# Attention and feed-forward block, one core: the FFN's first scale before the transposes of its tokens, one FFN tile before a V unit, evictions behind taps, and the next statistics in halves 4 and 5

## The chip, the cores and the metric

One core of a Trainium2 chip runs the whole block. The metric is the device time of an execution in microseconds, as the median of several runs. The engines are TensorE (PE in the profile, PEld its weight loads), VectorE (DVE), ScalarE (ACT), GpSimd (POOL) and SyncE (SP, which issues the DMAs); each runs its own list of instructions in order, and they wait on each other by semaphores.

## What is computed

64 sequences of 128 tokens and 256 channels pass cross-attention with a context of 192 channels (16 heads of 64; LoRA terms added to the weights; the last 4 context tokens have keys, values and a softmax of their own), then a feed-forward part with activations quantised to 8 bits and ternary weights.

```python
q_in = x @ Wq + lora(x);  k_in = org_ctx @ Wk + lora(org_ctx);  v_in = org_ctx @ Wv + lora(org_ctx)
out = attention(q_in, k_in, v_in) + attention(q_in, ipa_ctx @ Wk_ipa, ipa_ctx @ Wv_ipa)
x = x + (out @ Wo + bo + lora(out))              # of layernorm(x)
h = bit_linear(layernorm(x), w1)                  # 256 -> 1024; activations round(x*127/max|x|)
h = silu(depthwise_conv1d(h, conv_w) + conv_b)    # 3 taps along the tokens
x = x + bit_linear(h, w2)                         # 1024 -> 256
```

## The kernel before

The sequences go in 16 groups of 4 (NB = 4, so T = 512 tokens a group). Work is a software pipeline of passes; pass g has 32 halves, numbered n = 0 to 31. Pass g runs the attention of group g (one chunk of 4 heads and 1 sequence in every two halves: scores, softmax, transposes of the probabilities, p_v, output projection), the projections of group g+1 (functions `project`; the last of them, n + 32, lie in halves 0 to 7 of the next pass), and the feed-forward part of group g-1 (functions `finish`; its end, n + 32, lies in the pass after). Passes 0 and 1, and 15 to 17, are written out; 2 to 14 are a loop. The last group has its own `finish_last`.

Each engine has its own `steps(g, n)`, which calls the parts of half n in a fixed order; that order and the table of halves at the head of the file (N_... for projections, M_... for the feed-forward part) are all that sets the order of instructions. On TensorE a half is: on even n the four parts of the attention, then `project`, then `finish`. On ScalarE: on even n the copies of the attention's output and of the transposed probabilities, then `project`, then `finish`, then on even n the exponentials. On VectorE: on even n the sums of the chunk before, a copy of V, on even n the maxima, then `finish` of group g-2, `project`, `finish` of group g-1.

What the change touches:
- Layernorm of x: VectorE takes BN_STATS of XIN (line 877, two sequences a half, N_STATS), aggregates in half N_VAR = 5, POOL takes the power in half 6, VectorE normalises in half 7 (line 856). In halves 1 to 3 VectorE also scales and rounds the second activations (lines 1086, 1090).
- The first scale and the tokens' transposes: the bank psF is used in turn for the transposes of the quantised tokens Q1 (line 576, half M_QT = 13; ScalarE copies them into Q1T, line 764), for the transposes that lay the scales out along the tokens (line 582, half M_BC1 = 14; copied into BC, line 771), and then for the eight FFN tiles. The group before uses it until VectorE's line 1025 of half 11 (semaphore fin_done).
- The FFN tiles (line 591, halves 15 + M_TILE) all use psF: tile j waits until VectorE has evicted tile j-1 with BC as factor (line 1062, g_done). ScalarE then scales it into HT (line 777), VectorE adds the tap of the token before (conv_before, line 1003) and of the token behind (conv_next, line 997), ScalarE takes the tanh (line 782), VectorE the gate (line 1009).
- Units are projections of one tile: Q (line 443), K (452), V (462). p_v is line 478, the transposes of the probabilities are line 487, the scores 500, the output projection 513, the second FFN product 612. Softmax: maxima lines 913 and 914 and line 916 on VectorE, exponentials 751 and 754 on ScalarE, sums 906 and 908 on VectorE, product 1238 on POOL. POOL also runs lines 1269 and 1276.

In pass 6, which the rows below show, half 0 starts at 586.04 us, half 4 at 594.58, half 12 at 618.73, half 16 at 630.78, half 20 at 642.35 and half 28 at 662.70 (the first matmul of p_v in each); pass 7 starts at 675.10.

Of the kernel before, what the change touches and what calls it, by code (L numbers as in the profile page):

```python
# [44 lines left out]
CT = HID // P  # L45
# [8 lines left out]

N_STATS, N_VAR, N_POW, N_NORM = 0, 5, 6, 7
N_XT = 8
# [13 lines left out]
M_POW, M_NORM = 9, 9  # L70
M_QT, M_BC1 = 13, 14
M_F1 = 15
M_TILE = (0, 1, 2, 4, 5, 6, 8, 9)
M_LAG = (1, 1, 2, 3, 3)
M_HOFF = 4
M_HMAX = M_F1 + M_TILE[-1] + M_HOFF
M_HT, M_BC2 = M_HMAX + 2, M_HMAX + 4
# [69 lines left out]
def program(nc, x, ctxT, cipaT, Wq, Wk, Wv, Wo, bo, q_downT, q_up, k_downT, k_up, v_downT, v_up, o_downT, o_up,  # L147
            alphas, Wk_ipa, Wv_ipa, w1T, conv_w, conv_b, w2T, out):
    with ExitStack() as ctx:
# [269 lines left out]
        def _(pe):  # L419
# [146 lines left out]
            def finish(g, n):  # L566
# [3 lines left out]
                if n == M_QT:  # L570
                    pe.wait_ge(q1_done, g.count(1, 1))
                    need(pe, fin_done, g.count(2, 0))
                    bank = psF.bitcast(BF16).rearrange("p (k b t) -> p k b t", k=2, b=NB)
# [4 lines left out]
                if n == M_BC1:  # L578
                    pe.wait_ge(scale_done, g.count(2, 1))
                    pe.wait_ge(q1t_done, g.count(1, 1))  # L580
                    for b in range(NB):
                        m = pe.transpose(psF[:, TOK * b:TOK * b + TOK], AD[0][:, b:b + 1].broadcast_to([P, P]), IDF[:])
                    m.then_inc(bc_full, 1)
                j = tile_at(n - M_F1)
                if 0 <= j < CT:
                    if j == 0:
                        pe.wait_ge(bc_done, g.count(1, 1))
                    else:
# [89 lines left out]
            def steps(g, n):  # L678
# [8 lines left out]
                if g.reg is None:  # L687
                    ternary(g, n)
                if g.exists():
                    project(g, n + HALVES)  # L690
                if g.shift(1).exists(1):
                    project(g.shift(1), n)
                if g.shift(-2).exists():
                    finish(g.shift(-2), n + HALVES)
                if g.shift(-1).exists():
                    finish(g.shift(-1), n)
# [144 lines left out]
        def _(dve):  # L841
# [173 lines left out]
            def finish(g, n):  # L1015
# [30 lines left out]
                if n == M_NORM + M_SCALE:  # L1046
# [6 lines left out]
                    dve.wait_ge(q1_scaled, g.count(1, 1))  # L1053
                    dve.tensor_scalar(Q1, XN2, MAGIC, None, ALU.subtract).then_inc(q1_done, 1)
                j = tile_at(n - M_F1)
                if 0 <= j < CT:
# [5 lines left out]
                    dve.tensor_tensor(GB[j % 4].rearrange("p b t -> p (b t)"), psF, BC[:], ALU.mult).then_inc(g_done, 1)  # L1062
                j = tile_at(n - M_F1 - M_LAG[2])
                if 0 <= j < CT:
                    conv_next(g, j)
                j = tile_at(n - M_F1 - M_LAG[1])
                if 0 <= j < CT:
                    conv_before(g, j)
                j = tile_at(n - M_F1 - M_LAG[4])
# [254 lines left out]
```

## Time and profile before

| | |
|---|---|
| median of 3 runs | 1536.86 us (1536.23 to 1538.49) |
| profiled execution, its own time | 1535.5 us |
| its span, first to last instruction | 1533.5 us |
| TensorE busy | 1409.5 us, 92% |
| VectorE busy | 1195.5 us, 78% |
| ScalarE busy | 1182.3 us, 77% |
| POOL busy | 668.1 us, 44% |
| chain that ended last | TensorE 43%, VectorE 30%, ScalarE 17%, issue 9% |

The chain is followed back from the last instruction, at each step to what released it. Its shares say how long each engine set the end; "issue" is time in which an engine waited for nothing that the profile shows. Busy time of TensorE is modelled from pipelined matmuls, so starts are safer than ends. Times in the rows are us from the start of the span.

### The profile page before, as it was taken

To read this page: it belongs to the slowest core of one execution; us is meant where nothing else is said; L and a number is where in the kernel's file an instruction comes from. 1 tells how busy PE (TensorE), PEld (TensorE's weight loads), DVE (VectorE), ACT (ScalarE), POOL (GpSimd) and SP (SyncE) were. 2 spreads that over 40 slices of the span, in tenths; PEclk is the share of its full clock that TensorE was granted. 3 is DMA by queue.
4 is the path that set the end of the run, shared out by engine and by line. 5 is a ranking of instruction groups with operands and counts; after the bars stand their busy time and mean duration, and the time that the engine had idled before them with its cause. 6 is when DMAs were issued, how large, how long until landed. Compare 5 with 4: busy or idle time off the path is not lost.

```text
span 1533.5 us, 33070 instructions
## 1 busy us (share of the span) xinstructions
PE 1409.5 (92%) x10604; PEld 1159.5 (76%) x10650; DVE 1195.5 (78%) x3059; ACT 1182.3 (77%) x3909; POOL 668.1 (44%) x1058
## 2 busy tenths in 40 slices
PE   7899999999999999999999999999999999999762
PEld 4688778787777878777787878788787777878541
DVE  4363698787969878796887878688787878788888
ACT  3477787978878797887879788787978788797832
POOL 2354444445444444544544454444445444444420
PEclk9999999999999999999999999999999999999985
DMA  9210100000010100000010000001000000100000
GB/s 279 53 31 16 31 16 28 20 28 30 24 34 15 33 11 28 30 28 29 15 44 1 29 28 28 29 15 44 8 23 28 28 29 15 44 1 1 29 15 14
DMA packets 41144, 47.13 MB, mean 31 GB/s; under 512 B 3024, under 2 KB 35216, under 8 KB 41104
## 3 DMA queue, kind: packets, MB, share of 16 engines
q1 hardware_dynamic: 41104, 46.62, 10.1%
q8 instruction: 22, 0.36, 0.1%
q14 instruction: 18, 0.15, 0.0%
HBM read 36.13 MB, written 10.49 MB: 30 GB/s over the span
## 4 chain that ended last, share of the span: by engine, by line
PE 43%; DVE 30%; ACT 17%; issue 9%; DMA 1%; DVEq 0%; POOL 0%; SPq 0%; POOLq 0%; ACTq 0%
PE PS L500 10%; ACT SM L751 8%; PE PS L462 6%; PE PS L443 5%; PE PS L513 5%; PE PS L478 4%; PE PS L487 4%; PE PS L452 3%; PE PS L591 2%; DVE HP L1003 2%; DVE GBS L1062 2%; DVE MX L914 2%; DVE GBS L1086 2%; DVE HP L1009 2%; ACT QM L719 2%
## 5 line engine op out<-in xcount | busy, mean ns | idle before, releaser
L1238 POOL TENSOR_TENSOR SM<-SM,RC 128x496 f32<-128x496 f32 (+1 forms) x512 | 324.2, 654 | 738.6 <-DVE RC L908 738.6
L751 ACT ACTIVATE SM<-PS,MX 128x124 f32<-128x124 f32 x1024 | 359.9, 367 | 159.1 <-DVE SM L916 155.8
L500 PE MATMUL PS<-KT,QM 128*128 128x128 f32 x2048 | 278.1, 279 | 24.0 <-ACT SM L751 24.0
L500 PEld LDWEIGHTS PS<-KT,QM 128*128 128x128 f32 x2048 | 249.4, 192 | 38.6 <-ACT SM L751 38.1
L751 ACT ACTIVATION_READ_ACCUMULATOR SM<-PS,MX 128x1 f32 x1024 | 212.2, 207 | 0.0
L1269 POOL TENSOR_TENSOR OTl<-OF,OTh 128x256 fp32r<-128x256 f32 x256 | 204.1, 797 | 10.4 <-ACT OF L745 10.4
L487 PE MATMUL PS<-IDF,SM 128*128 128x128 f32 x1024 | 168.4, 287 | 16.6 <-POOL SM L1238 16.5
L743 ACT ACTIVATE OTh<-PS 128x256 fp32r<-128x256 f32 x256 | 100.4, 392 | 93.5 <-PE PS L478 92.5
L914 DVE TENSOR_REDUCE MX<-PS 128x4 f32<-128x496 f32 x256 | 170.5, 666 | 0.4 <-issue 0.4
L478 PEld LDWEIGHTS PS<-PT,V 128*64 128x64 f32 x2048 | 106.6, 136 | 82.3 <-issue 75.4
L478 PE MATMUL PS<-PT,V 128*64 128x128 f32 x2048 | 168.6, 286 | 0.0
L737 ACT ACTIVATE PT<-PS 128x512 f32<-128x512 f32 x256 | 157.4, 615 | 0.3 <-PE PS L487 0.3
L487 PEld LDWEIGHTS PS<-IDF,SM 128*128 128x128 f32 x1024 | 107.8, 141 | 63.1 <-issue 35.3
L1062 DVE TENSOR_TENSOR GBS<-PS,BC 128x512 f32<-128x512 f32 x120 | 82.5, 688 | 89.6 <-PE PS L591 88.6
L1009 DVE SCALAR_TENSOR_TENSOR HP<-GBS,HP 128x512 f32<-128x512 f32 x128 | 111.6, 872 | 22.0 <-ACT GBS L782 21.0
L513 PE MATMUL PS<-WOh,OTh 128*128 128x256 f32 x512 | 123.5, 322 | 0.7 <-POOL OTl L1269 0.7
L777 ACT ACTIVATE HP<-GBS,CB,CW 128x512 f32<-128x512 f32 x128 | 112.8, 882 | 10.0 <-DVE GBS L952 5.0
L913 DVE TENSOR_REDUCE MX<-PS 128x4 f32<-128x16 f32 x256 | 40.4, 158 | 100.6 <-PE PS L500 99.0
L997 DVE SCALAR_TENSOR_TENSOR HP<-GBS,CW,HP 128x508 f32<-128x508 f32 x128 | 110.0, 860 | 0.1
L443 PE MATMUL PS<-XTh,WQh 128*128 128x512 f32 x256 | 107.3, 419 | 0.0
L1003 DVE SCALAR_TENSOR_TENSOR HP<-GBS,CW,HP 128x508 f32<-128x508 f32 x128 | 97.3, 760 | 11.8 <-ACT HP L777 11.8
L745 ACT ACTIVATE OF<-PS 128x256 f32<-128x256 f32 x256 | 100.8, 394 | 5.4 <-POOL OTl L1269 5.4
(166 smaller groups left out, 3511.5 us busy)
## 6 DMA issues: line engine op xcount, KB each, us to landing
XIN<-in_x SPq DMA_DIRECT2D x16, 512.0 KB, 3.5
XRES<-in_x SPq DMA_DIRECT2D x16, 512.0 KB, 4.6
out_y<-HP SPq DMA_DIRECT2D x15, 512.0 KB, 3.2
CRAW<-in_ctxT SPq DMA_DIRECT2D x16, 256.0 KB, 2.7
RRAW<-in_ctxT SPq DMA_DIRECT2D x32, 128.0 KB, 2.9
QM<-in_Wq SPq DMA_DIRECT2D x1, 1024.0 KB, 9.1
GBS<-in_Wo SPq DMA_DIRECT2D x1, 1024.0 KB, 14.0
k_ipa_columns<-HP SPq DMA_DIRECT2D x1, 1024.0 KB, 6.5
```

The costliest lines, as they stand in the source:

```text
L443: m = mm(bank, WQ[w][:, k, P * tile:P * tile + P], XT[xt][:, k, :], start=(i == 0), stop=(i == 5))
L478: m = mm(psO[r:r + DH, h // 2, :], V[:, b, DH * (4 * q + h):DH * (4 * q + h) + DH], PT[:, h, :], start=True, stop=True)
L487: m = pe.transpose(psT[:, h, :], SM[c % 2][:, h, :], IDF[:])
L500: m = mm(psS[:, h, :], QM[:, 2 * q + h // 2, h % 2, TOK * b:TOK * b + TOK], KT[:, 2 * q + h // 2, b, :], start=True, stop=True)
L513: m = mm(psY[b // 2][:, b % 2, :], OT[ot][c % 2][:, a, :], WO[w][:, 2 * q + a, :], start=(q == 0 and i == 0 and b % 2 == 0), stop=(q == QU ...
L737: act.activation(PT[:], psT, ACT.Identity).then_inc(pt_done, 1)
L751: m = act.activation(SM[s % 2][:, h, 0:ORG], psS[:, h, 0:ORG], ACT.Exp, bias=MX[s % 2][:, h:h + 1], accum_out=SU[s % 2][:, h:h + 1])
L914: dve.tensor_reduce(MX[s % 2][:, 0:4], psS[:, :, 0:ORG], AX.X, ALU.max, negate=True)
L1003: dve.scalar_tensor_tensor(out=y[:, :, 1:TOK], in0=GB[j % 4][:, :, 0:TOK - 1], scalar=CW[:, j, 0:1], in1=y[:, :, 1:TOK], op0=ALU.mult, op1 ...
L1009: dve.scalar_tensor_tensor(out=y, in0=GB[j % 4], scalar=1.0, in1=y, op0=ALU.add, op1=ALU.mult).then_inc(h_done, 1)
L1238: m = pool.tensor_tensor(part, part, RC[c % 2][:, 4 * i:4 * i + 4].unsqueeze(2).broadcast_to(shape), ALU.mult)
L1269: pool.tensor_tensor(OT[1][c % 2][:], OF[:], OT[0][c % 2][:].bitcast(F32), ALU.subtract).then_inc(ot_done, 1)
```

## The change

Four edits to the order. The layout of the scales moves from half 14 to 12 (M_BC1), ahead of the tokens' transposes in 13, and the waits follow: the scales' transposes now wait for fin_done, the tokens' transposes for bc_done, the first tile for q1t_done. ScalarE's copy of BC follows to half 13, since it stands at M_BC1 + 1. In half 16 (M_AHEAD) TensorE runs `finish`, that is tile 1, ahead of `project`, the V unit. On VectorE the eviction of a tile stands behind conv_next and conv_before of the same half. BN_STATS of the next x moves from halves 0 and 1 to 4 and 5 (N_STATS).

```diff
--- before.py
+++ after.py
@@ -52,7 +52,7 @@
 U_Q, U_K, U_V = (0, 3), (1, 4), (2, 5)
 
 
-N_STATS, N_VAR, N_POW, N_NORM = 0, 5, 6, 7
+N_STATS, N_VAR, N_POW, N_NORM = 4, 5, 6, 7
 N_XT = 8
 N_CIN = 7
 N_CSPLIT = 8
@@ -68,11 +68,12 @@
 M_X2 = (4, 7)
 M_STATS = 7
 M_POW, M_NORM = 9, 9
-M_QT, M_BC1 = 13, 14
+M_QT, M_BC1 = 13, 12
 M_F1 = 15
 M_TILE = (0, 1, 2, 4, 5, 6, 8, 9)
 M_LAG = (1, 1, 2, 3, 3)
 M_HOFF = 4
+M_AHEAD = (16,)
 M_HMAX = M_F1 + M_TILE[-1] + M_HOFF
 M_HT, M_BC2 = M_HMAX + 2, M_HMAX + 4
 M_Q2 = M_HMAX + 5
@@ -569,7 +570,7 @@
                     return
                 if n == M_QT:
                     pe.wait_ge(q1_done, g.count(1, 1))
-                    need(pe, fin_done, g.count(2, 0))
+                    pe.wait_ge(bc_done, g.count(1, 1))
                     bank = psF.bitcast(BF16).rearrange("p (k b t) -> p k b t", k=2, b=NB)
                     for k in range(2):
                         for b in range(NB):
@@ -577,14 +578,14 @@
                     m.then_inc(q1t_full, 1)
                 if n == M_BC1:
                     pe.wait_ge(scale_done, g.count(2, 1))
-                    pe.wait_ge(q1t_done, g.count(1, 1))
+                    need(pe, fin_done, g.count(2, 0))
                     for b in range(NB):
                         m = pe.transpose(psF[:, TOK * b:TOK * b + TOK], AD[0][:, b:b + 1].broadcast_to([P, P]), IDF[:])
                     m.then_inc(bc_full, 1)
                 j = tile_at(n - M_F1)
                 if 0 <= j < CT:
                     if j == 0:
-                        pe.wait_ge(bc_done, g.count(1, 1))
+                        pe.wait_ge(q1t_done, g.count(1, 1))
                     else:
                         pe.wait_ge(g_done, g.count(CT, j))
                     for k in range(2):
@@ -686,13 +687,15 @@
                         project_out(g, 3)
                 if g.reg is None:
                     ternary(g, n)
+                if n in M_AHEAD and g.shift(-1).exists():
+                    finish(g.shift(-1), n)
                 if g.exists():
                     project(g, n + HALVES)
                 if g.shift(1).exists(1):
                     project(g.shift(1), n)
                 if g.shift(-2).exists():
                     finish(g.shift(-2), n + HALVES)
-                if g.shift(-1).exists():
+                if n not in M_AHEAD and g.shift(-1).exists():
                     finish(g.shift(-1), n)
 
             run_groups(pe, steps)
@@ -1052,6 +1055,12 @@
                     m.then_inc(q1_scaled, 1)
                     dve.wait_ge(q1_scaled, g.count(1, 1))
                     dve.tensor_scalar(Q1, XN2, MAGIC, None, ALU.subtract).then_inc(q1_done, 1)
+                j = tile_at(n - M_F1 - M_LAG[2])
+                if 0 <= j < CT:
+                    conv_next(g, j)
+                j = tile_at(n - M_F1 - M_LAG[1])
+                if 0 <= j < CT:
+                    conv_before(g, j)
                 j = tile_at(n - M_F1)
                 if 0 <= j < CT:
                     dve.wait_ge(f1_full, g.count(CT, j + 1))
@@ -1060,12 +1069,6 @@
                     if j >= 4:
                         dve.wait_ge(h_done, g.count(CT, j - 3))
                     dve.tensor_tensor(GB[j % 4].rearrange("p b t -> p (b t)"), psF, BC[:], ALU.mult).then_inc(g_done, 1)
-                j = tile_at(n - M_F1 - M_LAG[2])
-                if 0 <= j < CT:
-                    conv_next(g, j)
-                j = tile_at(n - M_F1 - M_LAG[1])
-                if 0 <= j < CT:
-                    conv_before(g, j)
                 j = tile_at(n - M_F1 - M_LAG[4])
                 if 0 <= j < CT:
                     gate(g, j)
```

VectorE at the start of a pass in the loop, from the end of half 0's softmax to the sums of half 2 (line 877 is BN_STATS, 906 the sums; in the changed file they are lines 880 and 909). Before:

```order
L916 TENSOR_TENSOR SM<-PS,MX 128x4x4
L875 REGISTER_ALU
L877 BN_STATS BS<-XIN 128x6 x2
L1083 ISA
L1086 TENSOR_TENSOR GBS<-HP,PS 128x512 x4
L1088 ISA
L1090 TENSOR_SCALAR HP<-GBS 128x512 x2
L1088 REGISTER_ALU
L1090 TENSOR_SCALAR HP<-GBS 128x512 x2
L877 BN_STATS BS<-XIN 128x6 x2
L906 TENSOR_REDUCE SU<-SM 128x4
```

Now:

```order
L919 TENSOR_TENSOR SM<-PS,MX 128x4x4
L1086 ISA
L1089 TENSOR_TENSOR GBS<-HP,PS 128x512 x4
L1091 ISA
L1093 TENSOR_SCALAR HP<-GBS 128x512 x2
L1091 REGISTER_ALU
L1093 TENSOR_SCALAR HP<-GBS 128x512 x2
L909 TENSOR_REDUCE SU<-SM 128x4
```

Both pairs of BN_STATS have left this stretch; they stand behind the softmax of half 4 and behind the copy of V in half 5.

ScalarE from the copy of Q1T in half 14 to the copy of BC in half 15 before (764 and 771), and from the exponentials of half 12 to the copy of Q1T in half 14 now (754, 774, 767). Before:

```order
L764 ACTIVATE Q1T<-PS 128x1024
L749 REGISTER_ALU
L751 ACTIVATE SM,SU<-PS,MX 128x124 x4
L754 ACTIVATE SM<-SM 128x4x4
L717 REGISTER_ALU
L718 ACTIVATE QM<-PS 64x512
L719 ACTIVATE QM<-PS 64x512
L769 ISA
L131 REGISTER_ALU
L771 ACTIVATE BC<-PS 128x512
```

Now:

```order
L754 ACTIVATE SM,SU<-PS,MX 128x124 x4
L757 ACTIVATE SM<-SM 128x4x4
L772 ISA
L132 REGISTER_ALU
L774 ACTIVATE BC<-PS 128x512
L746 ACTIVATE OTh<-PS 128x256
L748 ACTIVATE OF<-PS 128x256
L740 ACTIVATE PT<-PS 128x512
L767 ACTIVATE Q1T<-PS 128x1024
```

The copy of BC now stands right behind the exponentials of half 12, ahead of the copies of half 14; it stood behind the exponentials of half 14 and two copies of Q.

VectorE in halves 16 and 17, behind the softmax of half 16 (evictions 1062, now 1071; tap before 1003, now 1006; tap behind 997, now 1000). Before:

```order
L916 TENSOR_TENSOR SM<-PS,MX 128x4x4
L1057 REGISTER_ALU
L1062 TENSOR_TENSOR GBS<-PS,BC 128x512
L1003 SCALAR_TENSOR_TENSOR HP<-GBS,CW,HP 128x4x127
L1057 REGISTER_ALU
L1062 TENSOR_TENSOR GBS<-PS,BC 128x512
L997 SCALAR_TENSOR_TENSOR HP<-GBS,CW,HP 128x4x127
L1003 SCALAR_TENSOR_TENSOR HP<-GBS,CW,HP 128x4x127
```

Now:

```order
L919 TENSOR_TENSOR SM<-PS,MX 128x4x4
L1006 SCALAR_TENSOR_TENSOR HP<-GBS,CW,HP 128x4x127
L1066 REGISTER_ALU
L1071 TENSOR_TENSOR GBS<-PS,BC 128x512
L1000 SCALAR_TENSOR_TENSOR HP<-GBS,CW,HP 128x4x127
L1006 SCALAR_TENSOR_TENSOR HP<-GBS,CW,HP 128x4x127
L1066 REGISTER_ALU
L1071 TENSOR_TENSOR GBS<-PS,BC 128x512
```

The eviction of tile 1 moved behind one tap, that of tile 2 behind two.

## Rows read from the trace of the kernel before

**Rows 1.** The chain in order of time, passes 6 to 7: start, us, what.

```profile
605.04 0.17 DVE MX L913
...
645.68 0.49 DVE GBS L1062
...
651.78 0.07 ACT SM L751
```

**Rows 2.** Timeline of PE, one pass; in brackets idle us before, and its releaser.

```profile
624.83 1.16 PE L500 MATMUL PS<-KT,QM 128*128 128x128 f32 x8 [0.25 <-ACT SM L751]
...
630.47 0.38 PE L591 MATMUL PS<-Q1T,W 128*128 128x512 bf16 x1 [0.78 <-ACT BC L771]
...
636.02 0.60 PE L591 MATMUL PS<-Q1T,W 128*128 128x512 bf16 x2 [0.79 <-DVE GBS L1062]
...
663.70 0.66 PE L487 MATMUL PS<-IDF,SM 128*128 128x128 f32 x4 [0.34 <-POOL SM L1238]
...
665.18 1.16 PE L500 MATMUL PS<-KT,QM 128*128 128x128 f32 x8 [0.83 <-ACT SM L751]
...
684.78 0.66 PE L487 MATMUL PS<-IDF,SM 128*128 128x128 f32 x4 [0.49 <-POOL SM L1238]
...
685.77 1.16 PE L500 MATMUL PS<-KT,QM 128*128 128x128 f32 x8 [0.33 <-ACT SM L751]
```

**Rows 3.** Timeline, VectorE in halves 0 to 6: start, us, engine, line, op, out<-in.

```profile
588.97 0.74 DVE L877 BATCH_NORM_STATS2 BS<-XIN 128x6 f32<-128x256 f32 x2
...
593.35 0.76 DVE L877 BATCH_NORM_STATS2 BS<-XIN 128x6 f32<-128x256 f32 x2
...
594.01 0.16 DVE L906 TENSOR_REDUCE SU<-SM 128x4 f32<-128x16 f32 x1
...
605.04 0.17 DVE L913 TENSOR_REDUCE MX<-PS 128x4 f32<-128x16 f32 x1 [3.05 <-PE PS L500]
```

**Rows 4.** Timeline of all engines, halves 12 to 15.

```profile
621.33 0.87 DVE L1025 SCALAR_TENSOR_TENSOR HP<-PS,AD,HP 128x256 f32<-128x256 f32 x2
...
621.61 0.28 PE L462 MATMUL PS<-WVh,CTh 128*128 128x256 f32 x1
...
622.78 0.62 PE L576 MATMUL PS<-IDB,GBS 128*128 128x128 bf16 x8
...
624.66 0.22 ACT L754 ACTIVATE SM<-SM 128x16 f32<-128x16 f32 x1
...
627.93 0.60 PE L582 MATMUL PS<-IDF,AD 128*128 128x128 f32 x4
...
629.59 0.60 ACT L771 ACTIVATE BC<-PS 128x512 f32<-128x512 f32 x1
```

**Rows 5.** Timeline of ScalarE and VectorE, halves 16 to 20.

```profile
636.00 0.87 ACT L777 ACTIVATE HP<-GBS,CB,CW 128x512 f32<-128x512 f32 x1
...
638.33 0.85 ACT L777 ACTIVATE HP<-GBS,CB,CW 128x512 f32<-128x512 f32 x1
...
641.21 1.23 DVE L1009 SCALAR_TENSOR_TENSOR HP<-GBS,HP 128x512 f32<-128x512 f32 x1
...
643.73 0.68 DVE L1009 SCALAR_TENSOR_TENSOR HP<-GBS,HP 128x512 f32<-128x512 f32 x1
```

**Rows 6.** Timeline of PE: half 28 of pass 14, half 4 of passes 7, 15.

```profile
688.65 1.92 PE L612 MATMUL PS<-W,HP 128*128 128x256 bf16 x16
...
1377.43 1.16 PE L500 MATMUL PS<-KT,QM 128*128 128x128 f32 x8 [0.82 <-ACT SM L751]
...
1399.95 1.92 PE L612 MATMUL PS<-W,HP 128*128 128x256 bf16 x16
```

**Rows 7.** Timeline of PE late in pass 15, then busy time and clock by stretch.

```profile
1427.32 0.38 PE L591 MATMUL PS<-Q1T,W 128*128 128x512 bf16 x1 [1.67 <-ACT BC L771]
...
1441.63 0.61 PE L591 MATMUL PS<-Q1T,W 128*128 128x512 bf16 x2 [2.27 <-DVE GBS L1062]
...
1441.00:1446.00 5.00, 4.37 (x25) 3.61 (x26) 4.97 (x8) 4.71 (x15) 2.36 (x4) 0.66 0.00 0
```

## Prediction

> **What bounds the kernel now.** I read the busy shares and the chain that ended last on the page, then that chain in order of time over one pass, then TensorE's waits of the same pass, then the timeline of all engines around each wait. The chain changes hands within a pass [rows 1]: VectorE holds it from half 0 to the scores of half 4, takes it again with the maxima of half 6 (605.04) and keeps it until half 12, TensorE holds halves 14 to 19, VectorE comes back at 645.68, ScalarE takes over at 651.78 and runs without a pause into the scores of half 28. TensorE is busy nearly always, and what it loses is seven waits in each pass [rows 2]: 0.25 on the exponentials of half 12, 0.78 on the copy of the scales BC, 0.79 on the eviction of FFN tile 1, 0.34 and 0.83 in half 28 on the softmax of half 26, 0.49 and 0.33 in half 4 on the softmax of half 2. They sum to 3.81 us, and they recur, to a tenth or so, in each of the 13 passes 2 to 14. The change aims at five of the seven; the two of half 28 stand at the end of ScalarE's unbroken stretch, so whatever is late or early before them is settled there.
>
> **The change part by part**, in us per pass, in the times of the pass shown.
>
> *Statistics of the next x.* Two pairs of BN_STATS leave halves 0 and 1, 0.66 each from one start to the next (593.35 to 594.01; the first pair starts at 588.97) [rows 3]. Behind the second stand the sums of half 2 (594.01), on which POOL's product, and so the transposes of half 4, wait, and then maxima, exponentials and scores. The gain is at least 0.66 (the first pair may lie behind the broadcast of the scales, for which the products L1086 wait anyway) and at most 1.32. The trace has the very case: pass 15 has no next x, so no statistics in halves 0 and 1, and from the scores of half 28 to the second FFN product L612 it takes 1399.95 - 1377.43 = 22.52, where a full pass takes 688.65 - 665.18 = 23.47 [rows 2, 6]; none of the two waits stands there. I take 0.95. In halves 4 and 5 the same 1.32 runs before the maxima of half 6, where VectorE stands idle for 3.05 us now [rows 3], so I cost it at nothing. What covers it is that gap; without it the maxima of half 6, where VectorE's chain starts, would be later one for one. POOL's power of half 6 starts about 1 us later than now and is wanted only by L856 in half 7.
>
> *BC before Q1's transposes.* The 0.78 goes, but two waits come. Now the four transposes of the scales stand at the end of half 12 in the bank that the last pass's output still occupies: they wait for L1025, which ends at 621.33 + 0.87 = 622.2, while TensorE is there at 621.61: 0.6 [rows 4]. Behind them come the V unit (622.78 - 621.61 = 1.17) and Q1's transposes, now waiting for BC to be copied out, at about 622.2 + 0.4 + 1.17 = 623.8. That copy stands on ScalarE behind the exponentials of half 12 (the order rows on ScalarE), which end at 624.66 + 0.22 = 624.9; with 0.60 for the copy L771 TensorE goes on at 625.4: 1.6 of waiting. Q1's transposes thus start 2.6 late, and p_v, the transposes and the scores of half 14 are queued behind them on TensorE. Given back: the 0.25 (those exponentials are over by then), 0.36 of the 0.60 of L582 that leaves half 14, and the 0.78. At the scores of half 16 TensorE is 2.6 - 0.25 - 0.36 - 0.78, some 1.1 later than now; by starts instead of recorded waits 1.0. This part is a loss on TensorE. The bounds of the new wait: nothing, if the exponentials of half 12 came 1.6 earlier, and 1.6, which I take, since VectorE's chain from 605.04 to them is unbroken [rows 1] and no part of the change shortens it.
>
> *An FFN tile ahead of a V unit.* Tile 1 runs before the V unit of half 16, so the unit's 1.17 lies between it and tile 2. The 0.79 goes, less what the eviction is later: it now stands behind the first tap of tile 0, 0.74 alone or about 1.2 beside POOL. I take 0.4 as left.
>
> *Evictions behind taps.* In half 17 the eviction of tile 2 stands behind the tap of tile 1, which waits for ScalarE's scaling of tile 1. That scaling started at 636.00, when eviction 1 was done [rows 5]; with TensorE and the exponentials of half 16 about 1.0 late it starts near 636.8 and ends near 637.65; then a tap, then the eviction, done near 639.0; so ScalarE's scaling of tile 2 goes from 638.33 to about 639.05, and the exponentials of half 18 behind it, which had 0.1 to spare, are some 0.6 late. In half 20 VectorE waited 0.2 for a tile (the link at 645.68); now it waits for ScalarE's scaling of tile 3, 0.6 late, and the pair ends some 0.5 late. VectorE to 651.78 and ScalarE to 665.18 have no gap to make that up. So half 28 starts 0.55 late, and its two waits hide the rest of what TensorE lost. Bounds: 0.3, if the tap in half 16 runs alone and two small gaps take more, and 0.85, if the scaling waits for the whole lateness.
>
> *Sum.* Each of the 13 passes 2 to 14: -0.95 + 0.55 = -0.40, together -5.2. Pass 1 has the loss without the gain, +0.5; pass 15 has the loss in part and VectorE bound, +0.7. That is -4.0 against the profiled execution, 1535.5 to 1531.5; the median of the runs shown is 1.36 higher, so 1536.86 - 4.0 = 1532.9, say **1533**. With 0.3 and 0.85 it is -7.3 to -0.1, 1529.5 to 1536.8.
>
> **The rivals.**
>
> *Slower: the reordered taps meet POOL.* A gate L1009 takes 1.23 where it runs beside a POOL operation and 0.68 alone [rows 5]: 0.55 a meeting. Moving taps ahead of evictions shifts which of them fall beside POOL's L1269 and L1276. One more meeting on the way from half 16 to 651.78 makes the lateness 0.55 + 0.55 = 1.1, and each pass +0.15: 13 x 0.15 + 1.2 is +3.2, 1540; a second one gives another 7 us, 1547. It decides from a lateness of 0.95. For it: such meetings occur now, as at 641.21. Against it: a shift can also part a pair that meets now. The Trainium skill, "GPSIMD Engine Reference", section Specifications, says that POOL shares its SBUF interfaces with VectorE and that they contend where VectorE reads two SBUF inputs. By that rule taps and gates can be slowed and the evictions, which read PSUM, cannot; the trace agrees as far as 1.23 against 0.68 goes, and the rule gives no time of its own.
>
> *Handed back in full.* If half 28 is late by 0.95, ScalarE's stretch takes the whole gain: 1536.86 + 1.2, 1538.
>
> *Much faster: the wait for BC does not arise.* If the copy came before TensorE needs it, the 0.78 and most of 0.79 would go too, half 28 would be early by some 0.6, and a pass would save about 1.55: 13 x 1.55 is 20, 1517. Only ScalarE's order and the unbroken chain speak against it, but strongly.
>
> *Slower: the clock falls.* Behind a wait of 2.27 us (1441.63) TensorE's granted clock is 0.66 on average over the 5 us from 1441, a mixture of 2.4 and 1.2 GHz, and 0.34 x 5 = 1.7 us of work are lost; behind a wait of 1.67 the matmul at 1427.32 takes 0.38 as at 630.47, the full 2.4 GHz [rows 2, 7]. The new waits are 0.6 and 1.6 with work between. If the clock fell in each pass, 1.7 more of lateness would give 13 x (-0.95 + 2.25) + 1.2 = +18, 1555. The Trainium skill, "TensorE: Matmul & The Clock Gate", section Part 1: The HAM clock gate, says that the array's clock is half by default and that only activity releases it, and its section HAM oscillation — how this bites in real kernels warns of kernels that fall back between bursts; by that rule this rival can be, and the trace agrees in that the clock fell behind 2.27 and not behind 1.67.
>
> **How the numbers follow.** Forecast 0.58 (0.38 of it faster by over 0.2%, 3.07 us, which is about what can be told from no change here, and 0.20 within), meetings with POOL 0.17, handed back 0.11, no wait for BC 0.09, the clock 0.05. Faster 0.38 + 0.09 = 0.47, within 0.20 + 0.11 = 0.31, slower 0.17 + 0.05 = 0.22. The range leaves out the clock, the missing wait and the far end of the meetings: 1528 to 1545. The forecast's own range is 1529.5 to 1536.8.
>
> **What would show it.** In the profile after: no wait on POOL or ScalarE in half 4, and the next L612 some 0.95 sooner behind half 28; a wait of about 1.6 on ScalarE's BC before Q1's transposes and one of about 0.6 on L1025 before the scales' transposes, neither of which is there now; no wait before tile 0; a wait of 0.2 to 0.6 before tile 2; ScalarE still without a pause before half 28, and waits there of 0.0 to 0.3 (transposes) and some 0.8 (scores). The prediction is wrong if the wait on BC is under 1, if half 28 is late by more than 0.95 against half 6, or if TensorE's clock in the passes is under 1.00.

## The result, and the profile after

The changed kernel is slower: 1542.61 us median of 6 runs (1542.08 to 1544.32) against 1536.22 us for the kernel before, ratio 1.0044, 95% interval 1.0034 to 1.0053, or +6.4 us. The range (1528 to 1545) holds the time; the direction forecast (1533, faster) was wrong. The slower rival, taps meeting POOL, named 1540 for one more meeting and 1547 for a second.

The profiled execution after has a span of 1540.3 us, 6.8 above that of before. The page of the changed kernel, first its span and busy times, then the shares of the chain that ended last:

```profile
span 1540.3 us, 33070 instructions
PE 1413.3 (92%) x10604; PEld 1163.3 (76%) x10650; DVE 1221.5 (79%) x3059; ACT 1184.0 (77%) x3909; POOL 668.5 (43%) x1058
PE 44%; DVE 26%; ACT 19%; issue 9%; DMA 1%; POOL 0%; ACTq 0%; DVEq 0%; SPq 0%; POOLq 0%
```

VectorE is busy for 26.0 us more (1195.5 before), with the same 3059 instructions. The page's groups say where. Of the changed kernel, the two taps (1000 is conv_next, 1006 conv_before) and the gate (1012):

```profile
L1012 DVE SCALAR_TENSOR_TENSOR HP<-GBS,HP 128x512 f32<-128x512 f32 x128 | 110.5, 864 | 21.8 <-ACT GBS L785 20.5
L1006 DVE SCALAR_TENSOR_TENSOR HP<-GBS,CW,HP 128x508 f32<-128x508 f32 x128 | 111.4, 870 | 17.4 <-ACT HP L780 13.3
L1000 DVE SCALAR_TENSOR_TENSOR HP<-GBS,CW,HP 128x508 f32<-128x508 f32 x128 | 120.5, 942 | 0.1
```

and of the kernel before, the same taps (1003 and 997):

```profile
L997 DVE SCALAR_TENSOR_TENSOR HP<-GBS,CW,HP 128x508 f32<-128x508 f32 x128 | 110.0, 860 | 0.1
L1003 DVE SCALAR_TENSOR_TENSOR HP<-GBS,CW,HP 128x508 f32<-128x508 f32 x128 | 97.3, 760 | 11.8 <-ACT HP L777 11.8
```

The mean conv_before went from 760 to 870 ns and the mean conv_next from 860 to 942: 14.1 + 10.5 = 24.6 us of VectorE's 26.0.

TensorE's waits in pass 6 of the changed kernel, which answer to [rows 2] (timeline of PE, idle us before and releaser in brackets):

```profile
625.15 0.62 PE L583 MATMUL PS<-IDF,AD 128*128 128x128 f32 x4 [0.57 <-DVE HP L1028]
628.31 0.61 PE L577 MATMUL PS<-IDB,GBS 128*128 128x128 bf16 x8 [1.36 <-ACT BC L774]
634.34 0.38 PE L592 MATMUL PS<-Q1T,W 128*128 128x512 bf16 x1
639.62 0.60 PE L592 MATMUL PS<-Q1T,W 128*128 128x512 bf16 x2 [0.53 <-DVE GBS L1071]
650.60 0.61 PE L592 MATMUL PS<-Q1T,W 128*128 128x512 bf16 x2 [0.20 <-DVE GBS L1071]
667.68 0.65 PE L488 MATMUL PS<-IDF,SM 128*128 128x128 f32 x4 [0.37 <-POOL SM L1241]
669.16 1.16 PE L501 MATMUL PS<-KT,QM 128*128 128x128 f32 x8 [0.83 <-ACT SM L754]
```

Both waits of half 4 are gone, and so are those before the scores of half 14 and before tile 0. New are 0.57 for the bank before the scales' transposes and 1.36 for BC before Q1's transposes. Before tile 2 there is still 0.53, a wait of 0.20 has come before tile 5 (650.60), and the two waits of half 28 are nearly what they were (0.34 and 0.83). In pass 6 the granted clock is 1.00 (the stretch below gives the busy time of PE, PEld, DVE, ACT and POOL, then the granted clock, the DMA share and GB/s), and so it is in passes 2 to 14 before and after, so TensorE's clock is not part of what they cost:

```profile
589.70:679.00 89.30, 85.24 (x659) 71.09 (x660) 74.70 (x190) 72.85 (x245) 40.68 (x67) 1.00 0.08 25
```

The first matmuls of p_v give the length of each piece of the pass. In the changed kernel, the first p_v of halves 0, 4, 6, 12, 20 and 28 of pass 6 and of half 0 of pass 7 (timeline of PE; the counts are cut by the stretch asked for):

```profile
589.75 0.33 PE L479 MATMUL PS<-PT,V 128*64 128x128 f32 x2
598.29 0.44 PE L479 MATMUL PS<-PT,V 128*64 128x128 f32 x4
605.66 0.44 PE L479 MATMUL PS<-PT,V 128*64 128x128 f32 x4
621.52 0.44 PE L479 MATMUL PS<-PT,V 128*64 128x128 f32 x4
645.95 0.33 PE L479 MATMUL PS<-PT,V 128*64 128x128 f32 x2
666.65 0.55 PE L479 MATMUL PS<-PT,V 128*64 128x128 f32 x6
679.07 0.33 PE L479 MATMUL PS<-PT,V 128*64 128x128 f32 x2
```

The same starts in every run below give this table (pass 6, us between first matmuls of p_v; the other passes of the loop agree within 0.1 in their sum). "Median" is the run's own, of 4 to 11 executions, "ratio" that to the kernel before on the same chip, with its 95% interval. The kernel before took 1536.2 to 1537.5 on the chips used, so medians of two chips compare to about 1 us; the ratios are free of that.

| kernel | halves 4-5 | 12-15 | 16-17 | 20-21 | 28-29 | pass | median | ratio |
|---|---|---|---|---|---|---|---|---|
| before | 8.28 | 12.06 | 5.78 | 4.83 | 6.84 | 89.05 | 1536.22 | 1 |
| changed | 7.38 | 13.12 | 5.51 | 5.19 | 6.86 | 89.32 | 1542.61 | 1.0044 (1.0034-1.0053) |
| statistics alone | 7.32 | 12.06 | 5.78 | 4.83 | 6.78 | 88.08 | 1527.18 | 0.9937 (0.9923-0.9950) |
| scales first alone | 8.25 | 13.11 | 5.78 | 4.83 | 6.80 | 90.06 | 1552.74 | 1.0105 (1.0089-1.0120) |
| tile ahead alone | 8.24 | 12.07 | 4.85 | 4.83 | 6.81 | 88.10 | 1523.38 | 0.9912 (0.9897-0.9927) |
| taps first alone | 8.24 | 12.05 | 5.78 | 5.16 | 6.84 | 89.37 | 1541.16 | 1.0032 (1.0020-1.0045) |
| changed, BC copied in half 12 | 7.32 | 11.60 | 5.50 | 5.21 | 6.82 | 87.74 | 1518.80 | 0.9883 (0.9868-0.9898) |
| changed, evictions first again | 7.33 | 13.10 | 4.83 | 4.83 | 6.81 | 88.20 | 1528.69 | 0.9947 (0.9935-0.9960) |
| changed, additions late | 7.35 | 13.10 | 5.07 | 5.51 | 6.08 | 88.37 | 1532.31 | 0.9963 (0.9951-0.9976) |
| statistics and tile ahead | 7.37 | 12.06 | 4.83 | 4.83 | 6.82 | 87.17 | 1513.17 | 0.9845 (0.9832-0.9857) |
| best: the same and scales first, BC in 12 | 7.35 | 11.62 | 4.83 | 4.83 | 6.81 | 86.72 | 1503.38 | 0.9781 (0.9767-0.9794) |
| before, additions late | 8.24 | 12.05 | 5.78 | 4.83 | 6.78 | 88.98 | 1535.77 | 0.9992 (0.9983-1.0001) |
| best, additions late | 7.34 | 11.60 | 4.83 | 4.83 | 6.78 | 86.69 | 1504.07 | 0.9790 (0.9773-0.9808) |
| best, additions late, taps first | 7.33 | 11.62 | 5.07 | 5.49 | 6.10 | 86.91 | 1507.80 | 0.9810 (0.9796-0.9823) |

Of the 6.8 us between the two spans, 3.7 are passes 2 to 14 (1161.1 against 1157.4), 0.9 is pass 0, 0.8 pass 1, 1.2 pass 15, 0.8 lies before the first p_v and -0.6 behind pass 15. The 0.8 ahead of the first p_v is not the change's: over the runs here the first p_v starts anywhere between 82.6 and 84.0. Nor is it clear that the 1.2 of pass 15 is: there TensorE's granted clock is at its lower level (1.2 GHz) for 6.8 us, falling at 1448.6 during a wait of 2.55 for an eviction, and in the kernel before for 3.4 us, falling 0.8 behind the wait of 2.27 in [rows 7]; 3.4 us more at half the rate are 1.7 us of TensorE's work. No run here parts the two.

### The profile page after: what moved, and what is told of

Read it like the earlier page. It is cut to its first block, busy times and chain, and to the rows that moved or that the text cites. A ratio compares the mean times of both kernels' runs of the same rounds, so it can differ in the third digit from the quotient of the medians.

```text
span 1540.3 us, 33070 instructions
## 1 busy us (share of the span) xinstructions
PE 1413.3 (92%) x10604; PEld 1163.3 (76%) x10650; DVE 1221.5 (79%) x3059; ACT 1184.0 (77%) x3909; POOL 668.5 (43%) x1058
## 4 chain that ended last, share of the span: by engine, by line
PE 44%; DVE 26%; ACT 19%; issue 9%; DMA 1%; POOL 0%; ACTq 0%; DVEq 0%; SPq 0%; POOLq 0%
PE PS L501 8%; PE PS L444 7%; ACT SM L754 6%; PE PS L479 5%; PE PS L514 5%; PE PS L463 4%; PE PS L453 4%; PE PS L488 4%; DVE MX L917 2%; ACT HP L780 2%; DVE GBS L1071 2%; ACT GBS L785 2%; PE PS L613 2%; DVE HP L1012 2%; DVE HP L1006 2%
## 5 line engine op out<-in xcount | busy, mean ns | idle before, releaser
L1241 POOL TENSOR_TENSOR SM<-SM,RC 128x496 f32<-128x496 f32 (+1 forms) x512 | 331.9, 670 | 723.2 <-DVE RC L911 723.2
L1272 POOL TENSOR_TENSOR OTl<-OF,OTh 128x256 fp32r<-128x256 f32 x256 | 196.1, 766 | 18.5 <-ACT OF L748 18.5
L1006 DVE SCALAR_TENSOR_TENSOR HP<-GBS,CW,HP 128x508 f32<-128x508 f32 x128 | 111.4, 870 | 17.4 <-ACT HP L780 13.3
L1000 DVE SCALAR_TENSOR_TENSOR HP<-GBS,CW,HP 128x508 f32<-128x508 f32 x128 | 120.5, 942 | 0.1
```

The lines of the kernel that those rows point to most:

```text
L1006: dve.scalar_tensor_tensor(out=y[:, :, 1:TOK], in0=GB[j % 4][:, :, 0:TOK - 1], scalar=CW[:, j, 0:1], in1=y[:, :, 1:TOK], op0=ALU.mult, op1 ...
L1241: m = pool.tensor_tensor(part, part, RC[c % 2][:, 4 * i:4 * i + 4].unsqueeze(2).broadcast_to(shape), ALU.mult)
L1272: pool.tensor_tensor(OT[1][c % 2][:], OF[:], OT[0][c % 2][:].bitcast(F32), ALU.subtract).then_inc(ot_done, 1)
```

## Experiments, first set: each part alone

Four kernels, each the kernel before with one part of the change. Differences in this set are to the kernel before on the same chip (1536.33).

**Statistics alone.**

```diff
-N_STATS, N_VAR, N_POW, N_NORM = 0, 5, 6, 7
+N_STATS, N_VAR, N_POW, N_NORM = 4, 5, 6, 7
```

> The kernel before with one edit: BN_STATS of the next x in halves 4 and 5. Theory: the two waits of half 4 go and nothing hands them back, since VectorE and ScalarE from half 6 on take their start from half 4. In the changed kernel half 4 to half 6 took 7.36 us instead of 8.28, so 13 passes give 13 x -0.92 = -12.0; pass 0, where half 4 came 0.94 later in the changed kernel because VectorE is on the path there, gives +0.9. Sum -11.0, ratio about 0.9928. Rival, the gain is given back at half 28 or at the head of the next pass: -0.2 or less per pass, ratio 0.998 to 1.000.

Measured 1527.18, -9.2 us. Halves 4 and 5 take 7.32 instead of 8.28, nothing behind them moves, and a pass is 0.97 shorter. This part does what it was costed at in the loop. Pass 0 pays for it: from the first p_v to pass 1 it takes 63.15 instead of 62.20. In the profiled execution pass 1 takes 0.3 more and pass 15 1.6 more (80.57 for 78.94); pass 15 has 6.8 us at the lower clock here, 3.4 in the kernel before.

**Scales first alone.**

```diff
-M_QT, M_BC1 = 13, 14
+M_QT, M_BC1 = 13, 12
@@ tokens' transposes
-                    need(pe, fin_done, g.count(2, 0))
+                    pe.wait_ge(bc_done, g.count(1, 1))
@@ scales' transposes
-                    pe.wait_ge(q1t_done, g.count(1, 1))
+                    need(pe, fin_done, g.count(2, 0))
@@ tile 0
-                        pe.wait_ge(bc_done, g.count(1, 1))
+                        pe.wait_ge(q1t_done, g.count(1, 1))
```

> The kernel before with one edit: the scales laid out in half 12, ahead of the tokens' transposes, with the three waits that follow from it. Theory: TensorE waits about 1.4 for BC before the tokens' transposes and 0.6 for the bank before the scales' transposes, is 1.06 late at the scores of half 16, keeps the 0.79 wait before tile 2, and so starts half 18 about 1.0 late; ScalarE and VectorE had 0.1 to 0.3 to spare behind it, so half 28 is 0.7 to 1.0 late and each of 14 passes is 0.7 to 1.0 longer: +10 to +14, ratio 1.0065 to 1.009. Rival, that the wait costs nothing because half 28 is set by VectorE from half 20 on: 0.0 to +0.3 per pass, ratio 1.000 to 1.003.

Measured 1552.74, +16.4 us, more than the +10 to +14 expected: each of the 13 passes pays 1.05, pass 1 0.9, and pass 15, which the expectation left out, is 1.8 longer in the profiled execution (also with 6.8 us at the lower clock for 3.4). Halves 12 to 15 take 13.11 instead of 12.06, and all behind them is as long as before, the waits of half 28 included: the 1.05 is paid in full. Its new waits (timeline of PE):

```profile
627.65 0.62 PE L582 MATMUL PS<-IDF,AD 128*128 128x128 f32 x4 [0.58 <-DVE HP L1025]
630.82 0.61 PE L576 MATMUL PS<-IDB,GBS 128*128 128x128 bf16 x8 [1.37 <-ACT BC L771]
```

**Tile ahead alone.**

```diff
+M_AHEAD = (16,)
@@ TensorE, steps
+                if n in M_AHEAD and g.shift(-1).exists():
+                    finish(g.shift(-1), n)
...
-                if g.shift(-1).exists():
+                if n not in M_AHEAD and g.shift(-1).exists():
                     finish(g.shift(-1), n)
```

> The kernel before with one edit: FFN tile 1 ahead of the V unit of half 16. Theory: the wait of 0.79 before tile 2 goes, but the exponentials of half 18 stand behind other work of ScalarE with 0.1 us to spare and VectorE sets half 20, so 0.1 to 0.2 per pass is left: -1 to -3, ratio 0.998 to 0.999. Rival, TensorE sets the rest of the pass and the whole 0.79 is gained: -10, ratio 0.9933.

Measured 1523.38, -13.0 us: the theory fell, and even the rival's 0.79 a pass is exceeded. Halves 16 and 17 are 0.93 shorter and the whole of it stays. The reason is seen on VectorE. In the kernel before, this is the eviction of tile 1 (timeline of VectorE):

```profile
635.27 0.69 DVE L1062 TENSOR_TENSOR GBS<-PS,BC 128x512 f32<-128x512 f32 x1 [1.48 <-PE PS L591]
```

and with the tile ahead:

```profile
629.93 0.69 DVE L1065 TENSOR_TENSOR GBS<-PS,BC 128x512 f32<-128x512 f32 x1 [0.32 <-PE PS L592]
```

VectorE stood idle for 1.48 us before that eviction, waiting for TensorE's tile, and now for 0.32. The stretch of VectorE and ScalarE that ends in half 28 begins there, in half 16, and TensorE releases it. It is not a stretch of its own that would swallow what TensorE gains or loses before it.

**Taps first alone.**

```diff
+                j = tile_at(n - M_F1 - M_LAG[2])
+                if 0 <= j < CT:
+                    conv_next(g, j)
+                j = tile_at(n - M_F1 - M_LAG[1])
+                if 0 <= j < CT:
+                    conv_before(g, j)
                 j = tile_at(n - M_F1)
...
-                j = tile_at(n - M_F1 - M_LAG[2])
-                if 0 <= j < CT:
-                    conv_next(g, j)
-                j = tile_at(n - M_F1 - M_LAG[1])
-                if 0 <= j < CT:
-                    conv_before(g, j)
```

> The kernel before with one edit: on VectorE the eviction of a tile behind both taps of its half. Theory of the prediction: evictions wait behind the taps, ScalarE's scaling and the exponentials behind it come 0.3 to 0.85 later and half 28 with them: +4 to +11, ratio 1.003 to 1.007. Rival, the order alone costs nothing in the chain and only further meetings of taps with POOL's operations cost (a tap of 0.74 becomes 1.2; one on the path): 0.4 to 0.5 per pass and the mean tap of both kinds longer by 0.1: +5 to +7, with the exponentials of half 18 not later than before. The trace tells the two apart: where half 18 is late it is the first, where the lateness begins between half 20 and half 22 it is the second.

Measured 1541.16, +4.8 us. Halves 16 to 19 are as before and the lateness begins in halves 20 and 21 (5.16 for 4.83): the second of the two, not the path of the prediction through tile 2's scaling. The mean conv_before is 867 ns and the mean conv_next 941, as in the changed kernel, so this order alone lengthens the taps. How it does so is seen at tile 3. In the kernel before, POOL's second addition of the output bias (line 1276) runs beside the eviction of tile 3, which takes no longer for it (timelines of POOL and VectorE):

```profile
641.85 1.18 POOL L1276 TENSOR_TENSOR XRES<-XRES,BO 128x256 f32<-128x256 f32 x1
...
642.46 0.69 DVE L1062 TENSOR_TENSOR GBS<-PS,BC 128x512 f32<-128x512 f32 x1
643.07 0.74 DVE L997 SCALAR_TENSOR_TENSOR HP<-GBS,CW,HP 128x508 f32<-128x508 f32 x1
```

With taps first a tap stands in the eviction's place, takes 1.21 instead of 0.74, and the eviction comes 0.6 later in the pass (57.03 us into it instead of 56.42):

```profile
642.85 1.17 POOL L1276 TENSOR_TENSOR XRES<-XRES,BO 128x256 f32<-128x256 f32 x1
...
643.35 1.21 DVE L997 SCALAR_TENSOR_TENSOR HP<-GBS,CW,HP 128x508 f32<-128x508 f32 x1
644.48 0.68 DVE L1068 TENSOR_TENSOR GBS<-PS,BC 128x512 f32<-128x512 f32 x1
```

In half 16 a tap meets the first addition as well (1.20), but TensorE's tile 1 comes later still, so it costs nothing there.

The four medians add up to -9.2 + 16.4 - 13.0 + 4.8 = -1.0, and the change gave +6.4. Some 7 us come from the parts acting together.

## Experiments, second set: what eats the gains

**BC copied in half 12**, ahead of that half's exponentials on ScalarE; all else as in the changed kernel.

```diff
-                if n == M_BC1 + 1 and not is_last(g):
+                if n == M_BC1 and not is_last(g):
```

> The changed kernel with one edit: ScalarE copies BC in half 12, ahead of the exponentials of that half, instead of behind them. Theory: the wait of 1.36 us before the tokens' transposes is only ScalarE's order, so it goes, the exponentials of half 12 come about 0.2 late and meet nothing, and all that stands behind moves up: -1.1 to -1.4 in each of 14 passes, -15 to -19 against the changed kernel, 1523 to 1527. Rival, VectorE's chain from half 6 to 12 sets half 14 anyway: -0.3 or less per pass, 1538 or more.

Measured 1518.80, 24 us below the changed kernel, more than expected. Halves 12 to 15 fall from 13.12 to 11.60. The copy and the first of the exponentials, in the changed kernel (timeline of ScalarE; the exponentials end at 627.69):

```profile
626.08 0.36 ACT L754 ACTIVATE SM<-PS,MX 128x124 f32<-128x124 f32 x1 [0.60 <-DVE SM L919]
...
627.46 0.23 ACT L757 ACTIVATE SM<-SM 128x16 f32<-128x16 f32 x1
627.56 0.61 ACT L774 ACTIVATE BC<-PS 128x512 f32<-128x512 f32 x1
```

and with the copy ahead:

```profile
617.06 0.60 ACT L774 ACTIVATE BC<-PS 128x512 f32<-128x512 f32 x1 [0.41 <-PE PS L583]
617.55 0.36 ACT L754 ACTIVATE SM<-PS,MX 128x124 f32<-128x124 f32 x1
```

The copy stands in what was ScalarE's pause before the exponentials (0.60 in the changed kernel); they start 36.59 us into the pass (617.55 - 580.96) instead of 36.33 (626.08 - 589.75), 0.26 late, and nobody waits for that. The wait of 1.36 was ScalarE's order and nothing else: where it stands, scales first is a loss, and without it halves 12 to 15 are 0.46 shorter than in the kernel before.

**Evictions first again**: the changed kernel with the reordering of the taps undone (the diff of the taps above, the other way).

> The changed kernel with the edit of the taps undone (evictions ahead of both taps, as before); statistics, scales first and tile 1 ahead stay. By the single edits, which gave -9.2, +16.4 and -13.0, the sum is -5.8 against the kernel before, 1530. Theory: the order of the taps, not the scales, is what eats the gain of tile 1 ahead: the wait before tile 2 (0.53) goes and half 16 to 18 takes 4.85 instead of 5.51, half 20 to 22 takes 4.83 instead of 5.19; 1530, ratio 0.994 to 0.998. Rival, tile 1's gain is lost because the scales come late: half 16 to 18 stays near 5.5 and only the 0.36 of half 20 goes, 1537.

Measured 1528.69, ratio 0.9947, where the product of the three single ratios is 0.9953. Halves 16-17 and 20-21 both take 4.83. So the taps' order costs 13.9 us in the company of the other parts and 4.8 alone: 0.33 and 0.36 of a pass in half 20, and 0.68 in half 16 only where tile 1 comes early.

**Additions late.** In halves 16, 18, 20 and 22 POOL adds the output bias to the residual (line 1276, in the changed kernel 1279). Here it does so in halves 28 to 31, which have no taps and gates.

```diff
-                if n in (16, 18, 20, 22) and g.exists():
-                    b = (n - 16) // 2
+                if n in (28, 29, 30, 31) and g.exists():
+                    b = n - 28
```

> The changed kernel with one edit: POOL's four additions of the output bias to the residual (the operation that stands beside taps in halves 16 to 22) moved to halves 28 to 31, where no tap or gate runs. Theory, the price of the taps' order is meetings with POOL: taps of 1.2 on the path fall to 0.74, the wait of 0.53 before tile 2 falls to about 0.1 and half 20 to 22 from 5.19 to 4.83, so -0.6 to -0.8 per pass, 1532 to 1535. Rival, it is the order alone (the eviction behind a tap, whatever that takes): at most -0.2 per pass, 1540 to 1543.

Measured 1532.31, 10.3 us less by the medians and some 12 by the ratios. In the changed kernel, around tile 1 (timelines of VectorE and POOL):

```profile
637.77 1.19 DVE L1006 SCALAR_TENSOR_TENSOR HP<-GBS,CW,HP 128x508 f32<-128x508 f32 x1
638.89 0.68 DVE L1071 TENSOR_TENSOR GBS<-PS,BC 128x512 f32<-128x512 f32 x1
...
637.68 0.74 POOL L1279 TENSOR_TENSOR XRES<-XRES,BO 128x256 f32<-128x256 f32 x1
```

and with the additions late:

```profile
633.16 0.75 DVE L1006 SCALAR_TENSOR_TENSOR HP<-GBS,CW,HP 128x508 f32<-128x508 f32 x1
633.82 0.68 DVE L1071 TENSOR_TENSOR GBS<-PS,BC 128x512 f32<-128x512 f32 x1
```

The first tap of tile 0 stands ahead of the eviction of tile 1, and POOL's addition runs at the same moment: 1.19 instead of 0.75, the eviction later by as much, tile 2 behind it (the wait of 0.53). With the additions away, halves 16 and 17 are 0.44 shorter (5.07). The expectation for halves 20 and 21 was wrong, though: they are longer (5.51), with TensorE waiting there for an eviction (0.52) that stands behind a tap which waits for ScalarE:

```profile
644.44 0.77 DVE L1006 SCALAR_TENSOR_TENSOR HP<-GBS,CW,HP 128x508 f32<-128x508 f32 x1 [0.46 <-ACT HP L780]
645.13 0.68 DVE L1071 TENSOR_TENSOR GBS<-PS,BC 128x512 f32<-128x512 f32 x1
```

Half 28 gives more than that back (6.08 for 6.86), because VectorE is ahead by then: the eviction of tile 5 comes 62.73 us into the pass instead of 63.64. So what TensorE loses in halves 20 and 21 is not on the path to the end here. The expected mechanism is shown for half 16, where the same tap is seen with and without the addition, and for the pass as a whole; the lengths of the halves between are not a sum of meetings.

**Statistics and tile ahead**, the two parts that gain alone.

> The kernel before with two of the edits: statistics in halves 4 and 5, tile 1 ahead of the V unit. Theory, the two are on different stretches and both on the path: -9.2 - 13.0 = -22.2, 1514. Rival, with both gone another engine sets the pass (ScalarE from half 21 to 28 or VectorE from half 6 to 12) and a third or more of the second gain is lost: 1518 or more.

Measured 1513.17, ratio 0.9845, where the product of the two single ratios is 0.9850, and the pass is 1.88 shorter (0.97 + 0.95 alone). They add up; no third engine takes over.

## Experiments, third set: the best version, and a control

**Statistics, tile ahead, scales first with BC copied in half 12; evictions first.**

> The changed kernel with two edits: the order of evictions and taps undone, and BC copied in half 12 ahead of the exponentials. Theory: the early copy is worth here what it was worth in the changed kernel, -23.8 against the same kernel with the late copy (1528.7): 1505, some 8 below statistics and tile ahead alone (1513.2), so that laying the scales out first is a gain once the copy comes early. Rival: the early copy only takes back the loss of 16.4, and the kernel ends at 1511 to 1514.

Measured 1503.38, ratio 0.9781: 2.2% faster than the kernel before and, with the run below that only moves the additions, the best here. It is 9.8 below statistics and tile ahead alone, so with the early copy the scales first are a gain of their own, not only a loss taken back. TensorE has 1.7 us of waits left in a pass; before Q1's transposes there is none (timeline of PE):

```profile
612.44 0.62 PE L583 MATMUL PS<-IDF,AD 128*128 128x128 f32 x4 [0.59 <-DVE HP L1028]
614.08 0.62 PE L577 MATMUL PS<-IDB,GBS 128*128 128x128 bf16 x8
```

**The control: the kernel before with the additions late.**

> The kernel before with one edit: POOL's four additions of the bias to the residual in halves 28 to 31 instead of 16, 18, 20 and 22. This is the control for the same edit in the changed kernel, where it gave -10.3 (-0.95 a pass). Theory one, that gain was the price of the taps' order: here no tap on the path meets these additions but two gates of 1.22 and 1.23 do (0.55 each); where they are on the path at most -0.4 per pass, 1531 to 1537. Theory two, the additions cost as much whatever the order of the taps: -0.8 to -1.0 per pass here too, 1524 to 1526.

Measured 1535.77, ratio 0.9992 with 1 inside the interval. Where evictions come first, the additions cost nothing.

**The best version with the additions late, and the same with taps first.**

> Statistics in halves 4 and 5, scales first with BC copied in half 12, tile 1 ahead, evictions ahead of taps as before, and POOL's additions in halves 28 to 31. Against the same kernel with the additions in halves 16 to 22: by theory one (the additions cost only where taps come first) 0 to -5, by theory two -10 to -13.

> The same with evictions behind the taps: only the order on VectorE differs from the run beside it. If the price of that order is meetings with the additions, it is gone here and the two are within 3 us. If the order costs by itself (an eviction waits for a tap that waits for ScalarE), this one is 8 to 14 us slower.

Measured 1504.07 and 1507.80. The first is as fast as the best version (1503.38), so the control holds there too. The second says what is left of the taps' order once the additions are away: 3.7 us (a pass of 86.91 for 86.69), a little more than the 3 us expected of meetings alone and far from 8 to 14. With the additions in their place the order cost 1518.80 - 1503.38 = 15.4 on the same other edits. So 11.7 of 15.4, three quarters, goes when the additions are moved away. What the rest is stays open: the tap in front of an eviction still waits for ScalarE (0.46 to 0.78), and one tap of the pass now meets another POOL operation (line 1272; the same tap takes 0.78 with evictions first), here in timelines of VectorE and POOL:

```profile
647.64 1.28 DVE L1006 SCALAR_TENSOR_TENSOR HP<-GBS,CW,HP 128x508 f32<-128x508 f32 x1 [0.50 <-ACT HP L780]
...
647.64 0.74 POOL L1272 TENSOR_TENSOR OTl<-OF,OTh 128x256 fp32r<-128x256 f32 x1
```

## Why the prediction was wrong, step by step

*Statistics*: right. 0.95 was forecast, 0.92 came in the changed kernel and 0.97 alone. What it left out is pass 0: there VectorE has almost no gap in the halves that the statistics moved to, and the pass is 0.95 longer. The cover that the text named holds in the loop only.

*BC before Q1's transposes*: the waits were forecast as 0.6 and 1.6 and TensorE as 1.0 late at half 16; they are 0.57, 1.36 and 1.06. (The sum 2.6 - 0.25 - 0.36 - 0.78 is 1.2, not the 1.1 written there; the text went on with 1.0.) The step behind that failed: "VectorE to 651.78 and ScalarE to 665.18 have no gap to make that up. So half 28 starts 0.55 late, and its two waits hide the rest of what TensorE lost." They hid nothing: 0.37 and 0.83 against 0.34 and 0.83, and alone this part costs its whole 1.05. [rows 1] had said it: TensorE holds halves 14 to 19, so VectorE's stretch is released by TensorE. The row with which that stretch begins shows it, in the kernel before (timeline of VectorE):

```profile
645.68 0.69 DVE L1062 TENSOR_TENSOR GBS<-PS,BC 128x512 f32<-128x512 f32 x1 [0.22 <-PE PS L591]
```

Whatever TensorE loses up to there goes straight on to VectorE. What it gains goes on as well, by more than those 0.22, because VectorE's work before has the gap of 1.48 ten microseconds earlier, which TensorE ends too.

*Tile ahead*: mis-sized for the same reason. It was given 0.4 on TensorE; alone it is worth 0.95 a pass, and -13.0 us. That the eviction behind a tap would take part of it back was right: 0.53 was left before tile 2 where 0.4 was forecast, and halves 16 and 17 gain 0.27.

*Evictions behind taps*: the size was wrong, and the path. The text put 0.55 on a tap that waits for ScalarE and an eviction that makes ScalarE's scaling of tile 2 late. The tap does wait (0.34), but alone this part leaves halves 16 to 19 as they were. What it costs is 1.12 a pass here (89.32 - 88.20), by the eviction of tile 1 behind a tap that takes 1.19 beside POOL, and by halves 20 and 21. This is the mechanism of the slower rival: by it half 28 would be late by 1.1, and it is late by 1.16 against half 6 (666.65 - 605.66 = 60.99, and 662.70 - 602.87 = 59.83 before), beyond the 0.95 that the text gave as the point where it is wrong. That 1.1 and 1.16 agree is in part luck, since the parts differ: the rival has 0.55 and one meeting of 0.55, while with evictions first half 28 is 0.1 late (BC's 1.06 and tile 1's 0.95 nearly cancel) and the order of the taps adds the other 1.0. Stage by stage TensorE is 1.06 late at half 16 (1.0 in the text), 0.80 at half 18 (some 0.6) and 1.16 at half 22, where the text had about 0.5. The rival's evidence was [rows 5]; it was given 0.17, with the argument that a shift can as well part a pair that meets. In half 16 the new order does not shift a pair by chance: it moves the tap to the place right behind the softmax, where the addition stands.

*The sum*: -0.40 was forecast for each of 13 passes and +0.28 came. Of the 0.68 between them 0.03 is the statistics and 0.61 to 0.65 the lateness behind half 6 (1.16 at half 28, 1.18 to 1.20 at the end of the pass, for 0.55). The 13 passes are 8.9 us off, pass 0 0.9, passes 1 and 15 0.8 together.

*Direction and range*: the step that turned the direction is the order of the taps. It was costed as a tap that waits and an eviction behind it, with half 28 0.55 late in all; of taps held up beside POOL that counts at most the one in half 16 (the lower bound is for that tap alone), and a further one was left to the rival. Without that order the change gains (1528.69). The range held 1542.61 because it took in the near end of this rival, not because the forecast's sum was near.

*Clock, and the wait for BC*: in passes 2 to 14 the granted clock stayed at 1.00, and the wait came, as the forecast had it. The rival without that wait failed only by one line on ScalarE: with the copy in half 12 the changed kernel takes 1518.80, where the rival had 1517, and with evictions first as well 1503.38.

## What to carry to other kernels

Follow the stretch that sets the end back to where its engines last stood idle for long, and see who released them: what that engine lost or gained before was paid in full here (1.05 and 0.95 a pass), however unbroken the chain looked behind. What it loses behind that point need not be: of the time that halves 20 and 21 took longer with the additions late, half 28 gave back all. When a transpose or copy is moved ahead, move the copy that releases it as well, ahead of long work on its engine. Before putting VectorE operations that read two SBUF tensors on a path, look which GpSimd operations run at that time, and move the ones that have no hurry, or let an operation that reads PSUM stand there, as the evictions did in the kernel before.

## What the runs showed of the hardware

Where a tap or a gate runs beside one of POOL's tensor operations, the one that begins second is held up, and the one that begins first keeps its time. The addition of 637.68 begins 0.09 ahead of the tap of 637.77: the addition takes 0.74, as long as where nothing runs beside it (a mean of 732 ns with the additions late), and the tap 1.19 instead of 0.75. Later in the pass four such operations make a chain, in which each but the first is held up by the one that began before it (timelines of POOL and VectorE):

```profile
650.40 0.73 POOL L1272 TENSOR_TENSOR OTl<-OF,OTh 128x256 fp32r<-128x256 f32 x1
651.09 1.18 POOL L1279 TENSOR_TENSOR XRES<-XRES,BO 128x256 f32<-128x256 f32 x1
...
650.47 1.20 DVE L1012 SCALAR_TENSOR_TENSOR HP<-GBS,HP 128x512 f32<-128x512 f32 x1
651.60 1.22 DVE L1000 SCALAR_TENSOR_TENSOR HP<-GBS,CW,HP 128x508 f32<-128x508 f32 x1
```

Line 1272 comes first and takes 0.73; the gate begins 0.07 behind it and ends 0.54 after it (651.67 and 651.13); the addition begins during the gate and ends 0.60 after it; the tap begins during the addition and ends 0.55 after it. Evictions, which read one operand from PSUM, have a mean of 680 ns in the changed kernel and of 688 before, and the one beside an addition at 642.46 takes 0.69. The Trainium skill, "GPSIMD Engine Reference", section Specifications, says that POOL and VectorE contend where VectorE reads two SBUF inputs; the traces agree, with 0.44 us for the tap of 637.77. The Trainium skill's page "SBUF — State Buffer", section Who interferes with whom, calls what they share an exclusive lock and says that the order of issue decides who blocks. The traces agree with that as well: the first of two keeps its time, and the second ends 0.54 to 0.60 after the first however long the two overlap. That is 0.14 to 0.2 less than it takes alone (0.68 for the gate, 0.74 for the other two), so the hold-up is a little shorter than the overlap; why was not tried, and spans on POOL are rough.

What a meeting costs is set by where it falls: the same additions cost 10 to 12 us in the changed kernel, where taps ahead of evictions meet them, and nothing that can be measured in the kernel before, where an eviction or VectorE's idle time stands there.
